# A two-layer graph attention kernel: half of the next head's row products are issued ahead of a head's attention product, and the weights are split in another order

## What is computed

```
h = (x @ W).reshape(n, H, C)                       # rows of each head
e = leaky_relu(alpha_s[src] + alpha_d[dst], 0.2)   # alpha_s, alpha_d: h times a vector, per head
e = exp(e - segment_max(e, dst)[dst])
alpha = e / (segment_sum(e, dst)[dst] + 1e-16)
out = segment_sum(h[src] * alpha, dst) + b
```

## Time and profile before

| what | value |
|---|---|
| median of three runs | 640.87 us |
| the profiled execution | 641.08 us; its span from first to last instruction is 639.3 us, so 1.8 us lie around it |
| TensorE (PE) busy | 632.1 us, 99% of the span, 3426 matmuls |
| VectorE (DVE) busy | 518.9 us, 81% |
| ScalarE (ACT) busy | 337.8 us, 53% |
| GpSimd (POOL) busy | 204.4 us, 32% |
| mean granted TensorE clock | 0.998 of full speed |
| weight tiles (384 KB), issue to landing | 3.3 us in the median |

### The profile page before, as it was taken

One profiled execution on the slowest core, in us unless ns is written; L12 is line 12 of the kernel. 1 busy time (PEld: TensorE's weight loads), 2 busy tenths in 40 slices (PEclk: granted clock), 3 DMA queues, 4 the chain that ended last, 5 costly groups with the idle time before them and its releaser, 6 DMA issues.

```text
span 639.3 us, 9306 instructions
## 1 busy us (share of the span) xinstructions
PE 632.1 (99%) x3426; PEld 542.7 (85%) x3426; DVE 518.9 (81%) x928; ACT 337.8 (53%) x570; POOL 204.4 (32%) x122
## 2 busy tenths in 40 slices
PE   9999999999999999999999999999999999999996
PEld 6766568989888889988898889988998899887885
DVE  8999997889989987475855685567898589889876
ACT  7899992546524754353545454463545444534382
POOL 1000000140743630357124822374136604551230
PEclk9999999999999999999999999999999999999999
DMA  8422402115154420234113330316025401800002
GB/s 313 166 75 75 154 20 99 50 54 194 51 148 140 158 74 1 60 91 148 50 51 91 97 110 25 95 45 183 26 90 159 123 26 51 293 28 1 1 2 99
DMA packets 22173, 59.36 MB, mean 93 GB/s; under 512 B 2544, under 2 KB 2800, under 8 KB 22128
## 3 DMA queue, kind: packets, MB, share of 16 engines
q1 hardware_dynamic: 21984, 58.69, 28.6%
q10 hardware_dynamic: 144, 0.07, 0.0%
HBM read 54.03 MB, written 4.72 MB: 92 GB/s over the span
## 4 chain that ended last, share of the span: by engine, by line
PE 82%; DVE 16%; issue 1%; DMA 0%; ACT 0%; DVEq 0%
PE O L1238 30%; PE R L1136 8%; PE R L1133 8%; PE R L1139 8%; PE R L1205 6%; PE R L1211 6%; PE R L1208 6%; DVE ohd L679 4%; DVE ohs L683 2%; PE O L1150 2%; DVE junk L717 2%; DVE junk L736 2%; PE R L1155 1%; DVE W1l L705 1%; PE O L1205 1%
## 5 line engine op out<-in xcount | busy, mean ns | idle before, releaser
L1066 POOL TENSOR_TENSOR W2l<-Wr,W2h 128x768 fp32r<-128x768 f32 x48 | 93.3, 1953 | 207.8 <-ACT W2h L411 207.8
L1070 POOL TENSOR_TENSOR Pl<-L,Ph 128x512 fp32r<-128x512 f32 x34 | 54.0, 1599 | 166.7 <-ACT Ph L460 166.4
L1133 PE MATMUL R<-W1h,xTh 128*128 128x384 f32 x312 | 105.8, 339 | 0.0
L1139 PE MATMUL R<-W1h,xTl 128*128 128x384 f32 x312 | 104.9, 336 | 0.0
L1136 PE MATMUL R<-W1l,xTh 128*128 128x384 f32 x312 | 104.8, 336 | 0.0
L717 DVE CUSTOM_DVE_ANT_0 junk<-h,abc 128x768 bf16<-128x768 f32 x64 | 62.6, 978 | 41.8 <-ACT h L423 37.4
L1238 PE MATMUL O<-W2h,gh 128*128 128x256 f32 (+1 forms) x384 | 78.6, 339 | 0.0
L1238 PE MATMUL O<-W2h,gl 128*128 128x256 f32 (+1 forms) x384 | 77.4, 336 | 0.0
L1238 PE MATMUL O<-W2l,gh 128*128 128x256 f32 (+1 forms) x384 | 77.3, 335 | 0.0
L423 ACT COPY h<-R 128x384 f32<-128x384 f32 x62 | 29.5, 477 | 73.0 <-PE R L1139 70.9
L1060 POOL TENSOR_TENSOR W1l<-Wr,W1h 128x768 fp32r<-128x768 f32 x30 | 55.4, 1868 | 37.5 <-ACT W1h L400 37.5
(11 more groups left out here) (186 smaller groups left out, 1171.5 us busy)
## 6 DMA issues: line engine op xcount, KB each, us to landing
Wr<-in_W SPq DMA_DIRECT2D x101, 384.0 KB, 3.3
abc<-in_as SPq DMA_DIRECT2D x9, 384.0 KB, 4.0
abc<-in_ad SPq DMA_DIRECT2D x9, 384.0 KB, 5.9
h_rows<-h SPq DMA_DIRECT2D x8, 384.0 KB, 2.4
hl<-h_rows SPq DMA_DIRECT2D x8, 384.0 KB, 5.9
xin<-in_xT SPq DMA_DIRECT2D x6, 256.0 KB, 6.1
xr<-in_x SPq DMA_DIRECT2D x1, 1536.0 KB, 7.5
out<-res SPq DMA_DIRECT2D x4, 384.0 KB, 2.3
```

Of the source, the lines that this page charges most:

```text
L1066: e.tensor_tensor(W2l[:, m % N2, :], Wr[:, n, :], W2h[:, m % N2, :].bitcast(f32), ALU.subtract).then_inc(s_w2l, 1)
L1070: e.tensor_tensor(Pl[:, t, d0:d1], L[:, t, d0:d1], Ph[:, t, d0:d1].bitcast(f32), ALU.subtract).then_inc(s_Pl, 1)
L1133: e.matmul(bank[:, 0:HALF], xTh[:, f, xs], hi[:, ws], start=f == 0, stop=False)
L1139: m = e.matmul(bank[:, 0:HALF], xTl[:, f, xs], hi[:, ws], start=False, stop=f == FT - 1)
```

## The change

It moves B(h+1, 0..3) to a place between C(h-1, 4) and C(h-1, 5), ahead of A(h), for h = 2 to 6; B(h+1, 4..7) stay behind A(h). RING follows. The sums of the first two row tiles of the next head go ahead of `reciprocals(h)` on VectorE. The high and low parts of those two tiles (`high_h`, `low_h`) are put into c = 5 and behind it, since `hh` is free only after A(h). `high_w1(h+1, k)` moves from behind the scores to before and among them; `high_w2(h, 0..3)` moves from B(h+1) to c = 1 to 4 of A(h); `high_w2(h-1, 5)` moves behind the scores. GpSimd's order and the loads follow. The `products_W2` move one head earlier, in front of `reciprocals`.

```diff
-        LOADS += [("w2", h - 1, k) for k in range(FT)]
+        LOADS += [("w2", h - 1, k) for k in range(5)]
         LOADS += [("w1", h + 1, k) for k in range(FT) if h + 1 < H]
+        LOADS += [("w2", h - 1, 5)]
...
+    for h in range(EARLY, H + 1):
+        RING += [("B", h, n) for n in range(4) if h < H]
+        RING += [("den", h - 1, 0)] + [("A", h - 1, c) for c in range(FT)]
+        if h < H:
+            RING += [("B", h, n) for n in range(4, 8)] + [("as", h, 0), ("r2", h, 0), ("r1", h, 0)]
...
 # ScalarE, head h
-                    for t in range(NT):
+                    for t in (2, 3):
                         evict_B(h, t, 0)
-                        if t:
-                            high_w2(h - 1, t - 1)
                         evict_B(h, t, 1)
                         high_h(h, t)
                     scaled_as(h, 8 * h + 8)
-                    high_w2(h - 1, NT - 1)
+                    if h + 1 < H:
+                        high_w1(h + 1, 0)
+                        high_w1(h + 1, 1)
                     high_w2(h - 1, 4)
+                    scores(..., lambda u, h=h: high_w1(h + 1, 1 + u) if h + 1 < H and 1 <= u <= 4 else None)
+                    high_sums(h)
                     high_w2(h - 1, 5)
-                    scores(...)
-                    high_sums(h)
-                    for c in range(2, FT):
-                        if h + 1 < H:
-                            high_w1(h + 1, c - 2)
+                    if h + 1 < H:
+                        for t in range(2):
+                            evict_B(h + 1, t, 0)
+                            evict_B(h + 1, t, 1)
...
                 for c in range(FT):
+                    if c == FT - 1 and 2 <= h < H - 1:
+                        high_h(h + 1, 0)
                     exp_y(h, c)
                     if c:
                         high_g(h, c - 1)
+                    if c == FT - 1 and 2 <= h < H - 1:
+                        high_h(h + 1, 1)
...
-                    if EARLY <= h < H - 1 and c < 2:
-                        high_w1(h + 1, 4 + c)
+                    if 2 <= h < H - 1 and 1 <= c < 5:
+                        high_w2(h, c - 1)
...
 # VectorE, head h
-                    for t in range(NT):
-                        if t == 0:
-                            wait_abc(h)
+                    for t in (2, 3):
                         e.wait_ge(s_h32, 8 * h + 2 * t + 2)
                         sums_h(h, t, h32[:, t % 2, :], abc[:, abc_slot(h)[0], :, :])
                         low_h(h, t)
-                        if h - 1 in V_OF and t < 3:
-                            ...
-                            products_W2(V_OF[h - 1][t], 8 * h + 2 * t + 2)
...
+                if 2 <= h < H - 1:
+                    wait_abc(h + 1)
+                    for t in range(2):
+                        e.wait_ge(s_h32, 8 * (h + 1) + 2 * t + 2)
+                        sums_h(h + 1, t, h32[:, t, :], abc[:, abc_slot(h + 1)[0], :, :])
+                        if h in V_OF:
+                            ...
+                            for k in V_OF[h][0:1] if t == 0 else V_OF[h][1:3]:
+                                products_W2(k, 8 * (h + 1) + 2 * t + 2)
                 if h:
                     reciprocals(h)
...
+                    if c == FT - 1 and 2 <= h < H - 1:
+                        low_h(h + 1, 0)
                     if c > 1:
                         low_g(h, c - 2)
                     if c:
                         elu(h, c - 1)
+                if 2 <= h < H - 1:
+                    low_h(h + 1, 1)
                 elu(h, FT - 1)
...
 # GpSimd, head h
-                    for k in range(FT):
+                    for k in range(4):
                         low_w2(h - 1, k)
+                    if h + 1 < H:
+                        low_w1(h + 1, 0)
+                        low_w1(h + 1, 1)
+                    low_w2(h - 1, 4)
+                    if h + 1 < H:
+                        for k in range(2, FT):
+                            low_w1(h + 1, k)
                 for t in range(NT):
                     low_P(h, t, 0, N)
...
+                if h >= 2:
+                    low_w2(h - 1, 5)
...
 # TensorE, head h
-                    for n in range(8):
+                    for n in range(4, 8):
                         half_B(h, n // 2, n % 2, take("B", h, n))
...
                 for c in range(2 if h == 1 else 0, FT):
+                    if c == FT - 1 and 2 <= h < H - 1:
+                        for n in range(4):
+                            half_B(h + 1, n // 2, n % 2, take("B", h + 1, n))
                     stage_C(h - 1, c, between=(lambda h=h: denominators(h)) if c == FT - 1 else None, ...)
```

More of the change, by code:

```diff
@@ L51, in gat_resnorm_kernel @@
     RING += [("as", 2, 0), ("den", 1, 0)] + [("A", 1, c) for c in range(FT)]
[L52 to L55, removed]
+    RING += [("r2", 2, 0), ("r1", 2, 0)]
+    for h in range(EARLY, H + 1):
[3 more added lines that the diff above has]
+            RING += [("B", h, n) for n in range(4, 8)] + [("as", h, 0), ("r2", h, 0), ("r1", h, 0)]
     RING += [("al", H, 0), ("at", H, 0), ("as", H, 0), ("r2", H, 0), ("r1", H, 0), ("tail", 0, 0)]
@@ L335, in sync_program @@
             for h in range(EARLY, H):
-                if h + 1 < H:
-                    load_abc(h + 1 if h + 2 < H else H)
-                for k in range(FT):
+                if h + 2 < H:
+                    load_abc(h + 1)
+                for k in range(5):
                     load_raw("w2", h - 1, k)
-                if h + 2 == H:
-                    load_abc(H - 1)
                 if h + 1 < H:
@@ L344, in sync_program @@
                         load_raw("w1", h + 1, k)
+                        if k == 2 and h + 3 >= H:
+                            load_abc(H if h + 3 == H else H - 1)
+                load_raw("w2", h - 1, 5)
                 for k in V_OF.get(h, ()):
@@ L560, in scalar_program @@
                     high_w2(1, 4)
+                    high_w1(3, 3)
                     scaled_as(2, 24)
-                    scores(2, 2, 0, NT, ring_bank("r2", 2, 0), (gl_value(1, FT - 1), (s_g, 2 * FT)), 8, lambda u: high_w2(1, 5) if u == 3 else None)
+                    scores(2, 2, 0, NT, ring_bank("r2", 2, 0), (gl_value(1, FT - 1), (s_g, 2 * FT)), 8, lambda u: high_w1(3, 3 + u) if u in (1, 2) else None)
                     high_h(2, 0)
@@ L565, in scalar_program @@
                     high_sums(2)
+                    evict_B(3, 0, 0)
                     high_h(2, 2)
                     high_h(2, 3)
+                    high_w2(1, 5)
+                    evict_B(3, 0, 1)
+                    evict_B(3, 1, 0)
+                    evict_B(3, 1, 1)
                 if 0 < h < EARLY:
@@ L583, in scalar_program @@
                     scaled_as(h, 8 * h + 8)
-                    high_w2(h - 1, NT - 1)
+                    if h + 1 < H:
+                        high_w1(h + 1, 0)
+                        high_w1(h + 1, 1)
                     high_w2(h - 1, 4)
+                    scores(h, h, 0, NT, ring_bank("r2", h, 0), (gl_value(h - 1, FT - 1), (s_g, FT * h)), 3 * h + 2,
+                           lambda u, h=h: high_w1(h + 1, 1 + u) if h + 1 < H and 1 <= u <= 4 else None)
+                    high_sums(h)
                     high_w2(h - 1, 5)
-                    scores(h, h, 0, NT, ring_bank("r2", h, 0), (gl_value(h - 1, FT - 1), (s_g, FT * h)), 3 * h + 2)
-                    high_sums(h)
-                    for c in range(2, FT):
-                        if h + 1 < H:
-                            high_w1(h + 1, c - 2)
+                    if h + 1 < H:
+                        for t in range(2):
+                            evict_B(h + 1, t, 0)
+                            evict_B(h + 1, t, 1)
                     if h == H - 1:
@@ L714, in sums_h @@
                         e.wait_ge(s_asd, n)
-                    if not i and h - 1 in V_OF and t in range(1, 4):
-                        e.wait_ge(s_v, 2 * V_OF[h - 1][t - 1] + 2)
+                    if not i and h - 1 in V_OF and t in (1, 2):
+                        e.wait_ge(s_v, 2 * V_OF[h - 1][0 if t == 1 else 2] + 2)
                     e.tensor_tensor_reduce(
@@ L730, in products_W2 @@
                 for i in range(2):
-                    if i:
-                        e.wait_ge(s_v, 2 * k + 1)
+                    if i or k % 3 == 2:
+                        e.wait_ge(s_v, 2 * k + i)
                     else:
@@ L945, in vector_program @@
                         low_h(h, t)
-                        if h - 1 in V_OF and t < 3:
-                            if h == H - 2 and t == 0:
-                                wait_abc(H)
-                            products_W2(V_OF[h - 1][t], 8 * h + 2 * t + 2)
                     maxima(h, 0, NT, ring_bank("as", h, 0))
@@ L954, in vector_program @@
                         low_v()
+                if 2 <= h < H - 1:
[4 more added lines that the diff above has]
+                        if h in V_OF:
```

(13 more changed lines are left out.)

## The result

The changed kernel takes 705.35 us (median of four runs, 704.84 to 706.32) against 641.0 us of the kernel before in the same job: a ratio of 1.1006, 95% interval 1.0987 to 1.1025. It is slower by 64 us. The forecast was 691.8 us with a range of 668 to 705, so the time lies 0.35 us above the range. The profiled execution took 704.84 us; its span is 703.1 us.

What follows compares the result with a forecast made beforehand. TensorE, busy throughout heads 3 to 7, was taken to bound the kernel, with 0.3 us to give. Seam 42.0, reciprocals 5.4, targets 3.6, less 0.3, make 50.7 on 641.08: 691.8 us, range 668 to 705.

Steps and rivals of the forecast that it cites:

- What bounds the kernel: Heads 3 to 7: TensorE only issues matmuls, so reordering them can give back at most 0.3 us.
- The seam: A(h) to B(h+1, 4..7), five times: TensorE pauses 8.4 us, mostly before B(h+1, 6) awaiting ScalarE's eviction; 42.0 us.
- The step from the rows of A(1) to the new A(h): POOL's splits slow VectorE in A(h) as in A(1): 3.98 us from c = 4 to c = 5.
- the choice of 8.4 over 5.4 and 2.7: Pause before B(h+1, 6): 8.4 us worked out, 5.4 taking A(1) as it stands, 2.7 if POOL cost VectorE nothing.
- The reciprocals: A(5, 1) and A(6, 1) start 2.7 us late, as sums and products stand ahead of the reciprocal; 5.4 us.
- The targets: Heads 3 to 6: one small step behind the maxima blocked by POOL's three splits, 0.9 us each; 3.6 us.
- At nothing: Evictions of B(h+1, 0..3), W1's earlier use, loads, `low_w2(h-1, 5)` and `low_P`: hidden, no cost to TensorE.
- rival 4: W1 splits among the scores run 3 us later, B(h+1, 0) pauses 1.3 in five heads: 698 us; chance 0.07.
- rival 1: TensorE's clock falls in the five seam pauses, 1.9 us each, 9.5 more: 701 us; chance 0.22.
- Rivals 2 and 3: POOL blocks less than in A(1): 660 to 673 us, chance 0.18; TensorE stays full: 641 us, chance 0.06.
- rival 3: Not slower: two halves on A(h)'s last banks cover ScalarE's chain, TensorE stays full: 641 us; chance 0.06.

Runs made afterwards that it cites:

- the first experiment: Changed kernel with ScalarE evicting B(h+1, 4) and (h+1, 5) right behind exp_y of c = 5, not behind the last high_g: 677.15 us, ratio 1.0564.
- the second experiment: Changed kernel with the four W2 splits moved from A(h) to between the evictions of B(h+1, 4..7): 680.55 us, ratio 1.061.
- mended kernels: Changed kernel's TensorE order, with evictions, W2 and W1 splits and products moved: 647.67 us; against that, products and one W2 split moved again: 647.65 us.

## Why the prediction was wrong

**What bounds the kernel**: right. TensorE had 0.3 us to give (0.4 by the starts: before the targets of head 7 a matmul's start and the next transpose's stand 0.66 us apart, for a pace of 0.23), and no variant came below the kernel before.

**The seam**: right in place, order and size. Forecast 8.4 us in five seams, measured 7.9: 0.65 and 0.73 ahead of B(h+1, 4) and (h+1, 5) and 6.55 ahead of (h+1, 6). The step from the rows of A(1) to the new A(h) held (a pace of 3.97 for 3.98), and so did the choice of 8.4 over 5.4 and 2.7. That was no luck of two errors: in A(3), which starts at 319.70, `scale_A` of c = 5 starts 20.4 us later (forecast 20.5) and the first eviction, of 0.47 us, ends after 30.8 (forecast 31.1). The early eviction and the moved splits each took the share that the working gave to them.

**The reciprocals**: 2.85 measured for 2.7, twice, and gone when the products were moved; that of head 5 ends 5.55 us after the start of its A, for 5.4. **The targets**: 1.0 for 0.9 in heads 3 to 6, gone with one split, and head 7 without a pause. **At nothing**: W1, the loads and the first four evictions took no time from TensorE; rival 4 did not come up. Pauses in all: 49.2 for 51.0.

**The step that failed** is the one on the clock. The forecast took TensorE at the upper level throughout and left the fall to rival 1 at 0.22. The fall came, behind all five seams and once behind the pause before A(5, 1). Rival 1 also priced it too low: 1.9 us in five places, 9.5, from the program's first matmuls, where 2.2 on average in six places, 13.2, were measured. The filled pause settles the cause: with work in it the granted clock stays at 1.00 and the kernel is 10 us faster. So the sum of the pauses was right, and a cost that a pause can carry with it was left out. The 13.2 us make up the difference between 691.8 and the 704.84 of the profiled execution: the pauses came 1.8 shorter than forecast, and the small steps, which the forecast had at nothing, took about as much. The sentence against rival 1, that TensorE works on until two halves are through, was no reason: the row that could speak for the case was the only stretch in which TensorE had stood still, the start, and its starts, 0.42 us apart, showed the lower level.

Rivals 2 and 3 fell with the rows of the seam. Of rival 3 this much holds: with the lists mended, the two halves do cover the chain, since no wait for an eviction is left, but the time stays 1% longer.

## What to carry to other kernels

When one engine is full, as TensorE was here, a reordering of the same work has only that engine's last waits to win (0.3 us here) and can add many. Work out for each seam how long the other engines' lists are ahead of the release that the full engine needs, and count every instruction there that another engine can block at its blocked length. A pause of some microseconds on TensorE is then to be priced with the slow matmuls that can follow it, here 1.5 to 2.9 us more for each pause of 6.55. And expect repairs not to add up: three edits that each saved 9 to 28 us gave 22 together, since a cleared seam hands its lateness on.

## What was not expected of the hardware

The granted clock fell behind pauses much shorter than the 6.55 us of the seam. It did so behind the 2.85 us before A(5, 1) in the changed kernel, in the first experiment behind all four pauses of about 2.1 us before the targets, and in the second behind two of four such pauses and two of five of 2.3 us at the seam. The view by windows behind A(5, 1) of the changed kernel, and behind the targets of head 3 in the second experiment (the granted clock is the third number from the end):

```profile
485.30:489.40 4.10, 4.10 (x12) 3.31 (x13) 0.69 (x1) 0.72 (x1) 0.00 (x0) 0.64 0.00 0
```

```profile
284.40:289.00 4.60, 4.42 (x20) 3.99 (x21) 2.57 (x5) 3.74 (x7) 2.25 (x2) 0.63 0.82 276
```

Not every such pause did it. The one of 2.84 us before A(6, 1) in the changed kernel had no slow starts behind it, and in the kernel with one W1 split fewer neither of the two pauses of 2.85 us had. So the length of a pause alone does not decide at this size, and what does is open. In the mended kernels, with no pause over 1.6 us, no fall shows between the heads.
